# The first bf16 part of the keys is cast on ACT instead of DVE

## The chip, the cores and the metric

One core of one Trainium2 chip. The metric is the device time of one execution in microseconds. The kernel before took 319.92 us, median of three runs (319.9 to 320.2).

## The reference

Two layers over 32 sequences of 128 tokens with 128 features. All inputs are fp32.

```python
# layer 0: gated MLP with quantised activations and ternary weights
h = x * (scale[:, None, :] * rsqrt(mean(x * x) + 1e-6))      # scale = cond @ norm_w.T + 1
val, gate = split(h @ up_w.T, 2)
h = val * gelu(gate)
x = act_quant(h) @ weight_quant(down_w).T + x
...
# layer 1: attention with 16 heads of 8, and an MLP, both modulated by cond
h = layernorm(x) * g1 + b1
q, k, v = split(h @ W_qkv.T + b_qkv, 3)
attn = softmax(einsum('bhqd,bhkd->bhqk', q, k) / sqrt(8))
x = x + (einsum('bhqk,bhkd->bhqd', attn, v) @ W_o.T + b_o) * a1
x = x + (gelu_tanh((layernorm(x) * g2 + b2) @ W_f1.T + b_f1) @ W_f2.T + b_f2) * a2
```

## The kernel before, in words

The five engines each run an instruction list written out by hand; semaphores tie them together. There is no scheduler: what stands behind a waiting instruction on the same engine waits too.

The work has three parts. The first is layer 0, a pipeline of steps `s` (one sequence each, `gated_mlp(s)`). It also does the first layer norm of layer 1: POOL writes the normalised tiles (`xn_tile`, L1071), PE transposes them (L580), ACT modulates them into `feat` (L664). In a few steps listed in `EARLY_PROJ` PE projects four sequences at once to queries, keys or values: keys of group 0 in step 15 and of group 1 in step 23, values of group 0 in step 17. The second part is attention, one sequence `b` per step (`attention(b)`), in groups of four (GRP = 4) that share one projection each: queries in steps with b % 4 == 3, keys with b % 4 == 0, values with b % 4 == 2. The step with b % 4 == 1 has no projection. The third part is the MLP of layer 1, which PE fills.

Queries and keys are used as sums of bf16 parts. ACT saves a key projection as `k_f` (fp32, 128x512, L683). DVE casts it to the first part, `k_part[:, 0]` (`cast_k`, L818: a `tensor_tensor` addition of a zero that is broadcast). POOL takes the rest `k_rest` (L1026) and makes parts two and three of it (L1030, L1032). SP copies the parts by DMA into the stacked operands `k_st` (L301). Queries go the same way with a plain copy on DVE for the first part (L811), and L1016, L1018, L1022 on POOL. `cast_k` waits for the saved `k_f`, for the stacked rows of the group before (`k_stacked`), and for POOL's last part of the group before (`k_step`).

In an attention step PE computes two halves of the scores for the exponentials (`exp_scores`), the weighted values of one half of the step before and of one half of this step (`weigh`), two halves of the scores of the sequence three ahead for its maxima (`max_scores`), and a transposition of the split maxima (L434). DVE transposes the weighted values out of PSUM (`o_turn`, L900), takes the reciprocal (L903), reduces the two maxima (`mx`, L893) and transposes the normalised output back (L907). POOL splits the maxima into bf16 parts (L1040 to L1046) and multiplies by the reciprocals (`o_norm`, L1094). ACT runs the two exponentials (`probs`, L727), saves the projection between them if the step has one, and copies the transposed maxima (`m_T`, L743), which SP brings into the stacked queries (L349).

PE's matrix instructions are recorded by a helper, so most have line L274; they are told apart by their tiles (in the trace the moving operand stands first: `q_st,k_st` are scores for exponentials, `k_st,q_st` for maxima, `probs,v_pad` the weighting).

Of the kernel before, what the change touches and what calls it, by code (L numbers as in the profile page):

```python
# [10 lines left out]
ALU = mybir.AluOpType  # L11
# [3 lines left out]
P = 128  # L15
# [7 lines left out]
GRP = 4  # L23
GT = GRP * P
NG = B // GRP
# [7 lines left out]
STACKS = 3  # L33
# [40 lines left out]
def late_proj(b):  # L74

    name, ahead = {3: ("q", 9), 0: ("k", 8), 2: ("v", 2)}.get(b % GRP, (None, 0))
    g = (b + ahead) // GRP
    first = {"q": 2, "k": 2, "v": 1}.get(name, NG)
    return (name, g) if name and first <= g < NG else None
# [58 lines left out]
def build(nc, x, first, early, late, cond, out):  # L138
    x_d = x.rearrange("b t d -> t b d")
    out_d = out.rearrange("b t d -> t b d")  # L140
    with ExitStack() as ctx:
# [54 lines left out]
        zero_c, eps_c = sb("zero_c", [P, 1]), sb("eps_c", [P, 1])  # L196
# [85 lines left out]
        def k_done(g):  # L282
            return 16 * 6 * (g // STACKS + 1) + (CONST_DONE if g % STACKS else 0)
# [354 lines left out]
        def _(act):  # L638
# [28 lines left out]
            def save_projection(name, g):  # L667
                act.wait_ge(shared_mm, SHARED[name, g] + 1)
                if name == "v":
                    if g >= 2:  # L670
                        act.wait_ge(b_av, 2 * GRP * (g - 1))
                    if g == 0:
                        act.wait_ge(v_const_set, 2)
                    nc.scalar.copy(v_pad[:, g % 2, :, :, :].rearrange("p s j (i c) -> p (s j) i c", c=VPITCH // 4)[:, :, :, 0:DH],
                                   bank(MISC_BANK).rearrange("p (sj i d) -> p sj i d", i=4, d=DH)).then_inc(shared_set, 1)
                elif name == "q":
                    if g:
                        act.wait_ge(q_step, 3 * g - 2)
                    nc.scalar.activation(q_f[:, :], bank(MISC_BANK), ACT.Identity, bias=b_qk[:, 0:1]).then_inc(shared_set, 1)
                else:  # L680
                    if g:
                        act.wait_ge(k_step, 3 * g - 2)
                    nc.scalar.activation(k_f[:, :], bank(MISC_BANK), ACT.Identity, bias=b_qk[:, 1:2]).then_inc(shared_set, 1)  # L683

            def gated_mlp(s):
                if s + 1 < B:
                    scale_x(s + 1)
                if s < B:
                    n = s % 2
                    act.wait_ge(a_gate_mm, s + 1)  # L690
                    if s % GRP == 0:
                        act.wait_ge(rstd0_set, s // GRP + 1)
                    if s >= 2:
                        act.wait_ge(a_hid, s - 1)
                    nc.scalar.activation(gate[:, n, :], bank(1 + n), ACT.Gelu, scale=rstd0[:, s:s + 1]).then_inc(a_gate, 1)  # L695
                if s % GRP < 2 and s // GRP + 1 < NG:
                    g = s // GRP + 1
                    act.wait_ge(x_loaded[g], 16)
                    if g == 1:
                        act.wait_ge(ssq_set, GRP)  # L700
                    for e in range(2):
                        c = GRP * g + 2 * (s % GRP) + e
                        nc.scalar.activation(sq[:, (c % 4) * D:(c % 4 + 1) * D], tile_cols(x_tok, c), ACT.Square,  # L703
                                             accum_out=ssq[:, c:c + 1]).then_inc(sq_set, 1)
                if 0 <= s - 1 < B:
                    c, n = s - 1, (s - 1) % 2
                    act.wait_ge(a_qscale, c + 1)
                    if c >= 2:
                        act.wait_ge(a_hintT_mm, c - 1)
                    nc.scalar.activation(hrnd[:, n, :], hid[:, n, :], ACT.Copy, bias=ROUND_UP,  # L710
                                         scale=qscale[:, c % 4:c % 4 + 1]).then_inc(a_hrnd, 1)
                if 0 <= s - LN_LAG < B:
                    if s == LN_LAG:
                        act.wait_ge(mods_set, 6)
                    save_features(s - LN_LAG)
                if s in EARLY_PROJ:
                    if s == 13:
                        act.wait_ge(bias_set, 2)
                    save_projection(*EARLY_PROJ[s])

            def exps(b, r):
                n = 2 * b + r
# [8 lines left out]
            def attention(b):  # L731
                on, c = 0 <= b < B, b + LEAD - 1
                if on:
                    exps(b, 0)
                if late_proj(b):
                    save_projection(*late_proj(b))
                if on:
                    exps(b, 1)
                if 0 <= c < B:
                    act.wait_ge(shared_mm, SHARED["m", c] + 1)  # L740
                    if c >= 2:
                        act.wait_ge(m_stacked[c % 2], 16 * (c // 2))
                    nc.scalar.copy(m_T[:, c % 2, :], bank(MISC_BANK).bitcast(BF16)[0:HROWS, 0:P]).then_inc(shared_set, 1)  # L743
# [20 lines left out]
        def _(dve):  # L764
# [45 lines left out]
                    dve.wait_ge(q_step, 3 * g)  # L810
                v.tensor_copy(q_part[:, 0, :], q_f[:, :]).then_inc(q_cast, 1)  # L811

            def cast_k(g):
                dve.wait_ge(shared_set, SHARED["k", g] + 1)
                if g:
                    dve.wait_ge(k_stacked[(g - 1) % STACKS], k_done(g - 1))
                    dve.wait_ge(k_step, 3 * g)
                v.tensor_tensor(k_part[:, 0, :], k_f[:, :], zero_c[:, :].to_broadcast([P, GT]), ALU.add).then_inc(k_cast, 1)  # L818

            def gated_mlp(s):  # L820
                if 0 <= s - 2 < B:
                    c, n = s - 2, s % 2
# [58 lines left out]
                if s - 1 in EARLY_PROJ:  # L881
                    name, g = EARLY_PROJ[s - 1]
                    if name == "q":
                        cast_q(g)
                    if name == "k":
                        cast_k(g)

            def maxima(c, r):
                pair = PAIRS[OWNER[FILL_AT["max", c, r]]]
# [53 lines left out]
            def attention(b):  # L943
                if 0 <= b - 1 < B:
                    normalize(b - 1)
                if 0 <= b + LEAD < B:
                    maxima(b + LEAD, 0)
                g = (b + 8) // GRP
                if b >= 0 and b % GRP == 0 and g < NG:
                    cast_q(g)  # L950
                if b >= 0 and b % GRP == 1 and g < NG:
                    cast_k(g)
                if b == 27:
                    gate_projection(0)
                if b == 28:
                    add_residual(0, MISC_BANK)
                if 0 <= b + LEAD < B:
                    maxima(b + LEAD, 1)
                if 0 <= b - 1 < B:
                    turn_back(b - 1)  # L960
                if b == 28:
                    statistics(0)
                if b == 29:
                    gate_projection(1)
                if b == 30:
                    modulate(0, MISC_BANK)
                    add_residual(1, MISC_BANK)
                    statistics(1)
# [196 lines left out]
```

## Time and profile before

| | |
|---|---|
| median of three runs | 319.92 us |
| profiled execution | 319.64 us, span 317.8 us |
| mean granted clock of TensorE | 0.983 |
| PE busy | 279.6 us (88%) |
| DVE busy | 246.6 us (78%) |
| ACT busy | 186.3 us (59%) |
| POOL busy | 178.6 us (56%) |
| chain that ended last | PE 46%, POOL 20%, DVE 17%, issue 11%, ACT 4% |

The span runs from the first to the last instruction; the profiled execution's own time is 1.84 us longer. Busy shares are over the whole span and mix the three parts. The chain that ended last is followed back from the last instruction: at each step to what released it, or to the instruction before it on its engine. In the timeline a row has the start in us, the duration in us, engine, line, operation, tiles and shape; what stands in brackets is the idle time of the engine just before it and what ended that.

### The profile page before, as it was taken

Reading aid. Unit: us, or ns where it says so; the run is one execution under the profiler, and the core shown is the slowest. Engines: PE = TensorE matmul, PEld = TensorE weight load, DVE = VectorE, ACT = ScalarE, POOL = GpSimd, SP = SyncE. Lnnn points to the kernel's source line nnn. Section 1 sums busy time; section 2 is a strip of 40 time slices with the busy share of each in tenths; the row PEclk is TensorE's granted clock in tenths of the full one; section 3 lists DMA queues with packets and bytes.
Section 4 is the critical chain, followed back from the end, with each engine's and each line's share of the span. In section 5 each row is a group of like instructions: output and inputs, shape, how many; then the busy total and the mean of one; then the engine's idle time right before and its main releaser. Section 6 shows DMA issues by size and latency. Waiting matters only on the chain.

```text
span 317.8 us, 8220 instructions
## 1 busy us (share of the span) xinstructions
PE 279.6 (88%) x2892; PEld 154.6 (49%) x2892; DVE 246.6 (78%) x650; ACT 186.3 (59%) x347; POOL 178.6 (56%) x357
## 2 busy tenths in 40 slices
PE   3989998898989576999999989888877999999993
PEld 2454454454445344555656565655443455555441
DVE  5679997877899976598989898998955676676432
ACT  4557997687768564676677777675545222333330
POOL 8032684985896669377878696953334444322300
PEclk9999999999999997899999999999979999999999
DMA  7940000430340004335354444520000011011112
GB/s 238 327 102 4 0 1 3 120 87 2 92 116 2 0 10 113 86 78 143 93 142 104 119 108 112 149 72 8 6 3 3 0 33 33 1 35 33 33 35 66
DMA packets 26216, 21.57 MB, mean 68 GB/s; under 512 B 4384, under 2 KB 25536, under 8 KB 25920
## 3 DMA queue, kind: packets, MB, share of 16 engines
q1 hardware_dynamic: 25744, 20.37, 24.0%
q10 hardware_dynamic: 432, 0.67, 0.7%
q8 instruction: 24, 0.39, 0.6%
q14 instruction: 16, 0.13, 0.1%
HBM read 4.26 MB, written 2.10 MB: 20 GB/s over the span
## 4 chain that ended last, share of the span: by engine, by line
PE 46%; POOL 20%; DVE 17%; issue 11%; ACT 4%; DMA 1%; POOLq 0%; DVEq 0%; ACTq 0%
PE psum L274 39%; DVE mx L893 5%; POOL q_rest L1016 3%; POOL q_part L1018 3%; POOL q_part L1022 2%; POOL k_rest L1026 2%; DVE hid L838 2%; POOL o_norm L1094 2%; POOL xn_tile L1071 2%; DVE o_turn L900 1%; ACT sq L703 1%; PE psum L623 1%; DVE projT L912 1%; PE psum L460 1%; POOL m_rest L1042 1%
## 5 line engine op out<-in xcount | busy, mean ns | idle before, releaser
L893 DVE TENSOR_REDUCE mx<-psum 128x8 f32<-128x1024 f32 x64 | 75.9, 1193 | 10.5 <-PE psum L274 10.3
L727 ACT ACTIVATE probs<-psum 128x1024 f32<-128x1024 f32 x64 | 65.4, 1023 | 9.5 <-PE psum L274 7.9
L274 PE MATMUL psum<-w_early,h0T 128*128 128x512 f32 x128 | 69.3, 627 | 0.0
L760 ACT ACTIVATE g_act<-psum,w_late 128x512 f32<-128x512 f32 x32 | 22.0, 688 | 46.4 <-PE psum L274 46.4
L274 PE MATMUL psum<-probs,v_pad 128*32 128x128 f32 x1024 | 42.4, 285 | 3.3 <-DVE o_turn L900 2.8
L274 PE MATMUL psum<-h2T,w_late 128*128 128x512 f32 x64 | 31.3, 605 | 0.0
L274 PEld LDWEIGHTS psum<-probs,v_pad 128*32 128x32 f32 x1024 | 25.2, 111 | 11.0 <-ACT probs L727 4.4
L274 PE MATMUL psum<-g_act,w_late 128*128 128x512 f32 x64 | 28.8, 592 | 0.0
L838 DVE SCALAR_TENSOR_TENSOR hid<-psum,rstd,gate 128x512 f32<-128x512 f32 x32 | 23.7, 739 | 6.2 <-PE psum L274 3.7
L695 ACT ACTIVATE gate<-psum,rstd 128x512 f32<-128x512 f32 x32 | 22.0, 688 | 8.9 <-PE psum L274 8.5
L274 PE MATMUL psum<-q_st,k_st 64*128 64x128 bf16 x512 | 26.2, 224 | 0.6 <-DVE mx L893 0.5
L1071 POOL TENSOR_SCALAR xn_tile<-x_tok,mv,rstd 128x128 f32<-128x128 f32 x32 | 25.7, 809 | 1.7
L274 PE MATMUL psum<-k_st,q_st 64*128 64x128 bf16 x512 | 25.5, 220 | 0.6 <-DVE mx L893 0.6
L710 ACT ACTIVATE hrnd<-hid,qscale 128x512 f32<-128x512 f32 x32 | 22.9, 716 | 4.5 <-DVE qscale L864 4.3
L1059 POOL TENSOR_TENSOR ystep<-qstep,w_step 128x1 f32<-128x1 f32 x32 | 6.1, 192 | 31.5 <-DVE qstep L852 31.5
L840 DVE TENSOR_REDUCE amax<-hid 128x1 f32<-128x512 f32 x32 | 22.0, 686 | 1.1
L274 PEld LDWEIGHTS psum<-q_st,k_st 64*128 64x128 bf16 x512 | 15.2, 96 | 15.1 <-issue 11.4
L274 PEld LDWEIGHTS psum<-w_early,h0T 128*128 128x128 f32 x128 | 20.5, 200 | 3.1 <-issue 3.1
L274 PEld LDWEIGHTS psum<-k_st,q_st 64*128 64x128 bf16 x512 | 14.5, 94 | 13.5 <-issue 11.6
L994 DVE TENSOR_SCALAR yT<-psum,w_late,mods 128x128 f32<-128x128 f32 x32 | 10.9, 403 | 12.7 <-PE psum L274 12.7
L1100 POOL TENSOR_TENSOR var_e<-mv,eps_c 128x4 f32<-128x4 f32 x8 | 1.6, 201 | 33.7 <-DVE mv L932 33.7
L1094 POOL TENSOR_TENSOR o_norm<-o_turn,rinv 128x128 f32<-128x128 f32 x32 | 15.7, 491 | 7.9 <-DVE rinv L903 7.8
(125 smaller groups left out, 541.3 us busy)
## 6 DMA issues: line engine op xcount, KB each, us to landing
q_st<-q_part SPq DMA_DIRECT2D x48, 128.0 KB
k_st<-k_part SPq DMA_DIRECT2D x48, 128.0 KB, 2.4
x_tok<-x SPq DMA_DIRECT2D x8, 256.0 KB, 7.2
out<-out_t SPq DMA_DIRECT2D x8, 256.0 KB, 2.3
w_late<-late SPq DMA_DIRECT2D x1, 1159.5 KB, 9.1
w_early<-early ACTq DMA_DIRECT2D x2, 256.0 KB, 5.4
k_st<-k_st SPq DMA_DIRECT2D x4, 128.0 KB, 4.9
q_st<-q_st SPq DMA_DIRECT2D x4, 128.0 KB
```

What stands on the lines that cost most here:

```text
L274: return nc.tensor.matmul(o, w, m, start=start, stop=stop, skip_group_check=shares)
L695: nc.scalar.activation(gate[:, n, :], bank(1 + n), ACT.Gelu, scale=rstd0[:, s:s + 1]).then_inc(a_gate, 1)
L710: nc.scalar.activation(hrnd[:, n, :], hid[:, n, :], ACT.Copy, bias=ROUND_UP, scale=qscale[:, c % 4:c % 4 + 1]).then_inc(a_hrnd, 1)
L727: nc.scalar.activation(probs[:, n % 3, :, :, :].rearrange("p f j q -> p (f j q)"), psum[:, pair[0]:pair[1] + 1, :].rearrange("p a b -> p ( ...
L760: nc.scalar.activation(g_act[:, f, :], bank(2 + f % 2), ACT.Gelu_apprx_tanh, bias=wl("b_f1")[:, f:f + 1]).then_inc(c_gelu[f], 1)
L838: v.scalar_tensor_tensor(hid[:, n, :], bank(3 + n), rstd0[:, s:s + 1], gate[:, n, :], ALU.mult, ALU.mult).then_inc(a_hid, 1)
L840: v.tensor_reduce(amax[:, m:m + 1], hid[:, n, :], X_AXIS, ALU.max, apply_absolute_value=True).then_inc(a_amax, 1)
L893: v.tensor_reduce(mx[:, c % 2, :, r, :], psum[:, pair[0]:pair[1] + 1, :].rearrange("p f (j k) -> p f j k", j=4), X_AXIS, ALU.max, negate=T ...
L994: last = v.tensor_scalar(yT[:, s, :], bank(5)[:, s * P:(s + 1) * P], wl("b_f2"), mods[:, 5, b:b + 1], ALU.add, ALU.mult)
L1016: p.tensor_tensor(q_rest[:, :], q_f[:, :], q_part[:, 0, :], ALU.subtract).then_inc(q_step, 1)
L1071: p.tensor_scalar(xn_tile[:, n + e, :], tile_cols(x_tok, c + e), mv[:, n + e, 0:1], rstd[:, n + e:n + e + 1], ALU.subtract, ALU.mult).then ...
L1094: p.tensor_tensor(o_norm[:, :, :, :], o_turn[:, :, 0:16].rearrange("p g (e d) -> p g e d", e=2), rinv[:, :, :].unsqueeze(3).to_broadcast([ ...
```

## The change

`cast_k` moves from DVE to ACT. On DVE it was an addition of zero, on ACT it is a copy with a change of type. Its waits are the same. On ACT it stands at the end of step `s` of the first part where the step before projected keys (steps 16 and 24), and between the two exponentials of the attention step with b % 4 == 1.

```diff
+            def cast_k(g):
+                act.wait_ge(shared_set, SHARED["k", g] + 1)
+                if g:
+                    act.wait_ge(k_stacked[(g - 1) % STACKS], k_done(g - 1))
+                    act.wait_ge(k_step, 3 * g)
+                nc.scalar.copy(k_part[:, 0, :], k_f[:, :]).then_inc(k_cast, 1)
+
             def gated_mlp(s):
...
                     save_projection(*EARLY_PROJ[s])
+                if EARLY_PROJ.get(s - 1, "v")[0] == "k":
+                    cast_k(EARLY_PROJ[s - 1][1])
...
                 if late_proj(b):
                     save_projection(*late_proj(b))
+                if b % GRP == 1 and 2 <= (b + 7) // GRP < NG:
+                    cast_k((b + 7) // GRP)
                 if on:
                     exps(b, 1)
...
-            def cast_k(g):
-                dve.wait_ge(shared_set, SHARED["k", g] + 1)
-                if g:
-                    dve.wait_ge(k_stacked[(g - 1) % STACKS], k_done(g - 1))
-                    dve.wait_ge(k_step, 3 * g)
-                v.tensor_tensor(k_part[:, 0, :], k_f[:, :], zero_c[:, :].to_broadcast([P, GT]), ALU.add).then_inc(k_cast, 1)
...
-                    if name == "k":
-                        cast_k(g)
...
-                if b >= 0 and b % GRP == 1 and g < NG:
-                    cast_k(g)
```

ACT in a steady group of attention before, from the key projection's step (`k_f`) to that of the values (`v_pad`); `probs` are the exponentials, `m_T` the transposed maxima. In brackets the semaphores.

```order
L683 ACTIVATE k_f<-psum,b_qk 128x512 [waits k_step,shared_mm]
L727 ACTIVATE probs<-psum 128x1024 [waits b_av,b_s2]
L743 COPY m_T<-psum 64x128 [waits m_stacked0,shared_mm]
L727 ACTIVATE probs<-psum 128x1024 [waits b_av,b_s2] x2
L743 COPY m_T<-psum 64x128 [waits m_stacked1,shared_mm]
L727 ACTIVATE probs<-psum 128x1024 [waits b_av,b_s2]
L674 COPY v_pad<-psum 128x64x8 [waits b_av,shared_mm]
```

The same place now:

```order
L683 ACTIVATE k_f<-psum,b_qk 128x512 [waits k_step,shared_mm]
L736 ACTIVATE probs<-psum 128x1024 [waits b_av,b_s2]
L754 COPY m_T<-psum 64x128 [waits m_stacked0,shared_mm]
L736 ACTIVATE probs<-psum 128x1024 [waits b_av,b_s2]
L690 CAST k_part<-k_f 128x512 [waits k_step,k_stacked2,shared_set]
L736 ACTIVATE probs<-psum 128x1024 [waits b_av,b_s2]
L754 COPY m_T<-psum 64x128 [waits m_stacked1,shared_mm]
L736 ACTIVATE probs<-psum 128x1024 [waits b_av,b_s2]
L674 COPY v_pad<-psum 128x64x8 [waits b_av,shared_mm]
```

The two exponentials that ran one after the other have the cast with its three waits between them.

DVE at the same place before, from the query cast to the end of the step without a projection (`mx` are the maxima, `o_turn`, `rinv` and `feat` the output of the sequence before):

```order
L811 CAST q_part<-q_f 128x512
L893 TENSOR_REDUCE mx<-psum 128x2x4
L907 STREAM_TRANSPOSE feat<-o_norm 128x128
L900 STREAM_TRANSPOSE o_turn<-psum 128x256
L903 RECIPROCAL rinv<-o_turn 128x16
L893 TENSOR_REDUCE mx<-psum 128x2x4
L818 TENSOR_TENSOR k_part<-k_f,zero_c 128x512
L893 TENSOR_REDUCE mx<-psum 128x2x4
```

And now:

```order
L822 CAST q_part<-q_f 128x512
L895 TENSOR_REDUCE mx<-psum 128x2x4
L909 STREAM_TRANSPOSE feat<-o_norm 128x128
L902 STREAM_TRANSPOSE o_turn<-psum 128x256
L905 RECIPROCAL rinv<-o_turn 128x16
L895 TENSOR_REDUCE mx<-psum 128x2x4 x2
```

The two maxima of the step now stand side by side.

ACT at the end of step 16 of the first part, now (`h0T` and `gate` belong to the steps after):

```order
L717 ACTIVATE hrnd<-hid,qscale 128x512
L664 ACTIVATE feat<-psum,mods 128x128
L690 CAST k_part<-k_f 128x512
L655 ACTIVATE h0T<-psum,scale 128x128
L702 ACTIVATE gate<-psum,rstd 128x512
```

The row of the cast is new; before, `h0T` followed `feat`.

## Rows read from the trace of the kernel before

**Rows 1.** Instructions by tile (`k_part`, `o_norm`): ns min/median/max, first and last start.

```profile
L818 DVE TENSOR_TENSOR k_part<-k_f,zero_c x8: 672/676/802, 60.5 to 200.3; 128x512 bf16<-128x512 f32 x8
L1094 POOL TENSOR_TENSOR o_norm<-o_turn,rinv x32: 406/408/945, 122.6 to 243.3; 128x128 f32<-128x128 f32 x32
```

**Rows 2.** Chain of waits, 129 to 165 us: start, us on the chain, what.

```profile
155.92 0.69 POOL o_norm L1094
...
156.78 1.16 POOL q_part L1022
```

**Rows 3.** Timeline of attention, one steady group and the cast before it.

```profile
141.07 0.94 POOL L1094 TENSOR_TENSOR o_norm<-o_turn,rinv 128x128 f32<-128x128 f32 x1
...
153.33 1.02 ACT L727 ACTIVATE probs<-psum 128x1024 f32<-128x1024 f32 x1
...
154.54 1.02 ACT L727 ACTIVATE probs<-psum 128x1024 f32<-128x1024 f32 x1 [0.19 <-PE psum L274]
...
155.88 0.68 DVE L818 TENSOR_TENSOR k_part<-k_f,zero_c 128x512 bf16<-128x512 f32 x1
155.88 0.94 POOL L1094 TENSOR_TENSOR o_norm<-o_turn,rinv 128x128 f32<-128x128 f32 x1
...
156.26 0.26 ACT L743 COPY m_T<-psum 64x128 bf16<-64x128 bf16 x1 [0.69 <-PE psum L434]
...
156.48 0.64 PE L274 MATMUL psum<-probs,v_pad 128*32 128x128 f32 x16
...
159.38 0.40 PE L274 MATMUL psum<-k_st,q_st 64*128 64x128 bf16 x8
...
160.11 0.24 PE L434 MATMUL psum<-eye_b,m_part 128*64 128x128 bf16 x1 [0.33 <-POOL m_part L1046]
...
163.48 0.40 PE L274 MATMUL psum<-k_st,q_st 64*128 64x128 bf16 x8
...
163.81 0.24 PE L434 MATMUL psum<-eye_b,m_part 128*64 128x128 bf16 x1
```

**Rows 4.** Timeline of attention, the transposition behind the last key cast.

```profile
208.16 0.24 PE L434 MATMUL psum<-eye_b,m_part 128*64 128x128 bf16 x1 [0.82 <-POOL m_part L1046]
```

**Rows 5.** Timeline around step 16, and busy time per engine of one stretch.

```profile
59.03 0.71 ACT L710 ACTIVATE hrnd<-hid,qscale 128x512 f32<-128x512 f32 x1
...
59.64 0.44 ACT L664 ACTIVATE feat<-psum,mods 128x128 f32<-128x128 f32 x1
...
62.60 1.13 PE L274 MATMUL psum<-w_late,feat 128*128 128x128 f32 x8 [1.16 <-ACT feat L664]
...
63.77 0.59 ACT L674 COPY v_pad<-psum 128x512 f32<-128x512 f32 x1 [1.31 <-PE psum L274]
...
60.00:61.44 1.44, 1.44 (x11) 0.68 (x8) 1.44 (x8) 1.44 (x8) 1.34 (x2) 1.00 0.00 0
```

The last row's columns are the stretch, its length, busy us (and instructions) of PE, PE's weight loads, DVE, ACT and POOL, then the granted clock, the DMA share and GB/s.

**Rows 6.** Timeline of SP's issues, and landing times of the key rows.

```profile
150.29 0.54 SPq L301 DMA_DIRECT2D k_st<-k_part  x1
...
DMA to landing us min/median/max: 2.3/2.4/3.7
```

**Rows 7.** Layer norm tiles by tile (ns), and the timeline behind step 24.

```profile
L1071 POOL TENSOR_SCALAR xn_tile<-x_tok,mv,rstd x32: 795/799/995, 31.2 to 120.7; 128x128 f32<-128x128 f32 x32
...
93.28 0.33 PE L580 MATMUL psum<-w_first,xn_tile 128*128 128x128 f32 x1 [1.04 <-POOL xn_tile L1071]
...
93.64 0.46 ACT L664 ACTIVATE feat<-psum,mods 128x128 f32<-128x128 f32 x1 [0.98 <-PE psum L580]
```

**Rows 8.** PE's two longest waits in the timeline, and windows behind them (columns above).

```profile
122.68 0.32 PE L434 MATMUL psum<-eye_b,m_part 128*64 128x128 bf16 x1 [1.94 <-POOL m_part L1046]
...
231.55 0.22 PE L434 MATMUL psum<-eye_b,m_part 128*64 128x128 bf16 x1 [1.73 <-DVE projT L912]
...
122.50:129.20 6.70, 6.08 (x66) 4.32 (x66) 2.44 (x5) 2.92 (x5) 6.06 (x11) 0.50 0.39 104
231.70:235.10 3.40, 3.40 (x45) 2.25 (x48) 1.16 (x4) 1.44 (x3) 1.70 (x3) 0.50 0.02 5
```

## Prediction

> **What bounds the kernel now.** The granted clock and the span come first: one core, 317.8 us from first to last instruction, the profiled execution at 319.64 us, 0.28 below the median of the three runs (319.92). My sum is made against the execution and shifted by that 0.28 at the end. Then the chain of waits, then the timeline of one group of four attention steps, then the timeline around the two early casts; the windows by stage give the clock.
>
> The cast that moves runs eight times on DVE, 0.68 us each [rows 1]: twice in the first part of the kernel (steps 16 and 24 of the gated MLP), six times in attention, in the step with b % 4 == 1. DVE is busy there, but the chain of waits of a steady group does not pass through the cast. It passes through POOL: the query remainder and its second part, the split of a maximum, then the o_norm multiplication, which stands with 0.69 us on the chain, the third query part at 156.78 [rows 2], the first key remainder, the split of the next maximum, and from there to PE's transposition at 160.11, for which PE stood 0.33 us [rows 3]. Group follows group at 14.81 us: the o_norm beside the cast starts at 155.88 here and at 141.07 one group earlier [rows 3].
>
> The reader should see one pair in the timeline: the cast on DVE and o_norm on POOL start together at 155.88, and o_norm takes 0.94 us [rows 3] where the fastest takes 0.41 and the median is 0.41 too [rows 1]. So the cast costs POOL 0.53 us in the place where POOL is on the chain. The Trainium skill (SBUF — State Buffer, section Who interferes with whom) says that VectorE and GpSimd share a port pair as an exclusive lock, also when a VectorE instruction has two SBUF inputs and the other reads SBUF; by that rule the loser waits out the whole 0.68 us of the cast. The row says 0.53 and decides; with 0.68 only the last group below would gain 0.15 more.
>
> **The change, part by part.**
>
> *Removed from DVE: eight casts of 0.68 us.* As DVE time I cost this at nothing in attention: the second maximum of step b % 4 == 2, like those of steps 3 and 0, starts when PE has filled its banks, so a freer DVE waits for PE. What counts is POOL. Without the cast beside it o_norm ends 0.53 us sooner, and the third query part, the key remainder and the split behind it with it. PE's transposition at 160.11 follows. It cannot gain all of it: PE's own last scores started at 159.38, and where PE does not wait, a step later, a transposition starts 0.33 us after such scores (163.48, 163.81) [rows 3]. So it can start at 159.71: **0.40 us per group**. Bounds: the idle time that the row itself gives, 0.33, and POOL's whole 0.53. Late next is PE's own stream; in steps 3 and 0 all three projections keep PE back to back, DVE and ACT follow it, and the chain returns through DVE's maximum, the query cast and POOL's query remainder, all earlier by the same 0.40. Four groups (casts near 141, 156, 171 and 185 us) give 1.60. The last (200.3 us) has no query projection behind it: there PE waits 0.82 us for POOL at 208.16 [rows 4], so the whole **0.53** passes. The first (121 us) has no stretched o_norm, since POOL is at the layer norm tiles there; I put it at 0. Sum for attention: 1.60 + 0.53 = **2.13 us less**.
>
> *Added to ACT in attention: six casts between the two exponentials.* No row has ACT casting from SBUF. The nearest are the copy of the values from PSUM, 0.59 us, and hrnd, SBUF to SBUF with a scale, 0.71 us, whose successor starts 0.61 after it [rows 5]; the copy is nearest, since it has no scale from a tile, and with the 0.10 by which neighbours overlap it keeps ACT for about 0.5. Ends: 0.49 and 0.61. The first exponential starts at 153.33, the second at 154.54 after 0.19 of idle, and 0.69 us before the maximum's copy at 156.26 ACT idles again [rows 3]. So the second exponential comes some 0.3 us later and ends near 155.9; the weighting that reads it starts at 156.48, the copy is due at 156.26. Both are covered. If the cover were gone, each further tenth would fall on PE five times.
>
> *The wait that comes with it.* On ACT the cast waits for the landing of the previous group's last key rows, and the second exponential, the copy of the maximum and through them PE are queued behind it. That transfer is issued at 150.29 and key rows land 2.3 to 3.7 us after issue [rows 6], by 154.0 at the latest; the cast comes at about 154.25 (after an exponential of 1.02 us from 153.33, less the overlap of 0.10). Nothing, so long as landings stay under 3.9 us. POOL takes the result up only behind the third query part, and SP behind query rows of its own, so neither gains or loses by an earlier cast.
>
> *Added to ACT at step 16.* Here nothing covers it. ACT is busy 1.44 of 1.44 us between 60.00 and 61.44 [rows 5], and PE stands 1.16 us for ACT's feat before the value projection at 62.60 [rows 5]. The cast goes in ahead of all that ACT work, so PE starts later by its whole price: **0.5 us more** (0.49 to 0.61). DVE's 0.68 us gained there buys nothing, since its next product needs ACT's gate, which comes later.
>
> *Step 24.* Here a layer norm tile of POOL runs beside the cast and takes 0.995 us, the longest of its kind, where the median is 0.799 [rows 7]. POOL goes on back to back until PE's transposition at 93.28, for which PE stands 1.04 us [rows 7]. I take **0.2 us less** (0.995 - 0.799). ACT is 0.5 us later here too, but it waits 0.98 us itself before the feat at 93.64 [rows 7], which covers that. Bounds: 0.2 less, 0.5 more if that cover fails.
>
> **Sum:** 319.64 - 2.13 + 0.50 - 0.20 = 317.81 against the profiled execution; with 0.28 for the median, **318.1 us**. Bounds by the ends: all five groups at 0.53 and ACT at 0.49 give 319.92 - 2.65 + 0.49 - 0.20 = 317.6; four groups at 0.33, ACT at 0.61 and step 24 at 0.5 more give 319.92 - 1.85 + 1.11 = 319.2.
>
> **Rivals.**
> (a) *TensorE's clock falls at step 17; slower.* The granted clock is 0.5 (1.2 of 2.4 GHz) from 122.5 to 129.2 and from 231.7 to 235.1, each time after PE had stood still for long, 1.94 and 1.73 us [rows 8]. At 62.60 PE now stands 1.16 us and the clock stays up; with 0.5 more it stands 1.66. [...] In the first part PE is busy all through, so a stretch of 3.4 to 6.7 us at half clock loses half of itself, 1.7 to 3.35 us: 319.8 to 321.4, middle 320.6. For it: 1.66 is nearer to 1.73. Against: the step before is fuller than those before 120 and 230.
> (b) *The gain in attention does not come, slower by the first part alone.* If o_norm still took 0.94 beside the maximum that now follows at once on DVE, 319.92 + 0.5 = 320.4. Against: other o_norms run at 0.41 beside maxima.
> (c) *The clock does not fall at 122.5.* PE's 1.94 us of standing there ends a little sooner with a freer POOL; without the fall half of 6.7 us is gained on top: 314.7. Against: 1.94 is well above 1.73.
> (d) *Part of the gain is taken back*, by a late landing in front of the second exponential or by SP, which carries all of the queries' and keys' rows: two groups of five lost, 0.8 us, 318.9.
> (e) *ACT is slow at it.* If the cast kept ACT for 2.0 us, the second exponential would end after the weighting's 156.48; past 1.1 us (0.19 + the 0.92 from 155.56 to 156.48) every tenth is on PE. At 2.0: PE 0.9 late, less the 0.40 gained, five times, plus 2.0 at step 16: 324.4. Against: ACT's 512-wide rows take 0.59 to 0.71. [...]
>
> **How the numbers follow.** Forecast 0.58, (a) 0.19, (b) 0.05, (c) 0.07, (d) 0.09, (e) 0.02. A measurement of this kernel can tell about 0.2%, 0.64 us, from no change. The range 317.2 to 320.6 takes in the forecast with its bounds and some spread, (d), (b) and the shorter half of (a); outside stay (c), (e) and the longer half of (a), 0.19 together. The forecast's own range is 317.4 to 319.2. Faster by over 0.2% (below 319.3): the forecast, (c) and most of (d), 0.72. Within 0.2%: the shorter half of (a), (b) and the edge of (d), 0.16. Slower (above 320.6): the longer half of (a) and (e), 0.12.
>
> **What would show it.** Right: o_norm at 0.41 in every group, groups 14.4 us apart instead of 14.81, no PE wait before the transposition of step 2, an ACT cast of about 0.6 us, and the value projection of step 17 half a microsecond later after 1.66 us of standing at an unbroken clock. Wrong: a granted clock of 0.5 soon after 63 us, an exponential that waits for key rows, o_norm still at 0.9, or PE waiting in attention for ACT's second exponential.

## The result and the profile after

The changed kernel takes **317.60 us** (median of 10 runs, 315.94 to 318.35), the kernel before 319.98 us on the same chip (10 runs, 318.78 to 320.82). The ratio is 0.9919, with a 95% interval of 0.9895 to 0.9944. Ratios here and below leave out executions in a slower state of the chip, and they differ by up to 0.4% from the quotients of the medians. The prediction was 318.1 us, range 317.2 to 320.6.

| | before | after |
|---|---|---|
| profiled execution, span | 319.64 us, 317.8 us | 316.87 us, 315.1 us |
| mean granted clock of TensorE | 0.983 | 0.987 |
| steady groups of the attention apart | 14.81 us | 14.41 us |

First the instructions by tile (ns min/median/max, first and last start), to be read against [rows 1, 7]:

```profile
L690 ACT CAST k_part<-k_f x8: 606/610/619, 59.9 to 197.1; 128x512 bf16<-128x512 f32 x8
...
L1094 POOL TENSOR_TENSOR o_norm<-o_turn,rinv x32: 405/406/408, 122.6 to 240.5; 128x128 f32<-128x128 f32 x32
...
L1071 POOL TENSOR_SCALAR xn_tile<-x_tok,mv,rstd x32: 792/795/800, 31.1 to 120.8; 128x128 f32<-128x128 f32 x32
```

The cast takes 0.61 us on ACT. What counts is the third number of the other two rows. The longest of 32 `o_norm` was 0.945 us and is 0.408; the longest layer norm tile was 0.995 and is 0.800. Neither line of POOL was touched by the change. A group's median would have hidden it: the medians, 0.408 and 0.799 before, are 0.406 and 0.795 now.

Then the timeline of one steady group, to be read against [rows 3]:

```profile
152.98 1.02 ACT L736 ACTIVATE probs<-psum 128x1024 f32<-128x1024 f32 x1
...
153.90 0.61 ACT L690 CAST k_part<-k_f 128x512 bf16<-128x512 f32 x1
...
154.41 1.03 ACT L736 ACTIVATE probs<-psum 128x1024 f32<-128x1024 f32 x1
154.45 2.29 DVE L895 TENSOR_REDUCE mx<-psum 128x8 f32<-128x1024 f32 x2
...
155.53 0.41 POOL L1094 TENSOR_TENSOR o_norm<-o_turn,rinv 128x128 f32<-128x128 f32 x1
...
155.91 0.26 ACT L754 COPY m_T<-psum 64x128 bf16<-64x128 bf16 x1 [0.48 <-PE psum L434]
...
156.13 0.64 PE L274 MATMUL psum<-probs,v_pad 128*32 128x128 f32 x16
```

The cast keeps ACT for 0.51 us (153.90 to 154.41, since neighbours overlap by 0.10). The exponential behind it ends at 155.44, 0.69 us before the weighting that reads it and 0.47 us before ACT's next copy. The cast is covered. And the chain of waits of the same stretch (start, us on the chain, what):

```profile
155.36 0.23 POOL m_part L1046
155.59 0.04 issue
155.63 0.24 PE psum L434
155.87 3.56 PE psum L274 x72
159.43 0.17 PE psum L434
```

Before, the chain went on through `o_norm`, the third query part and the first key remainder on POOL to the next transposition [rows 2, 3]. Now it stays on PE for 3.56 us, and the transposition at 159.43 follows PE's own scores without a wait. PE's transpositions behind POOL stand at 155.63, 170.04 and 184.44, 14.41 and 14.40 us apart.

Timeline at the two early casts and behind the last, to be read against [rows 4, 5, 7]:

```profile
63.02 1.13 PE L274 MATMUL psum<-w_late,feat 128*128 128x128 f32 x8 [1.67 <-ACT feat L664]
...
93.46 0.33 PE L580 MATMUL psum<-w_first,xn_tile 128*128 128x128 f32 x1 [0.54 <-POOL xn_tile L1071]
...
206.03 0.24 PE L434 MATMUL psum<-eye_b,m_part 128*64 128x128 bf16 x1 [0.44 <-POOL m_part L1046]
```

At step 17 PE stands 1.67 us for ACT's `feat`, 0.51 more than before; at step 24 0.54 us for POOL's tile (1.04); and behind the last cast 0.44 us for POOL (0.82). The granted clock (windows, the column after POOL):

```profile
62.00:70.00 8.00, 6.98 (x42) 4.16 (x43) 5.53 (x19) 5.84 (x12) 6.84 (x11) 1.00 0.40 108
...
122.00:130.00 8.00, 6.87 (x75) 4.65 (x75) 2.41 (x6) 3.31 (x5) 6.41 (x13) 0.57 0.36 96
...
134.00:226.00 92.00, 86.74 (x1732) 54.61 (x1731) 82.39 (x141) 67.93 (x98) 62.48 (x158) 1.00 0.38 99
226.00:240.00 14.00, 9.22 (x152) 5.50 (x151) 8.51 (x33) 7.03 (x9) 7.24 (x13) 1.00 0.02 4
```

Behind the wait at step 17 the clock stays at 1.00. The fall at PE's long wait near 122 us is there as before. The second, from 231.7 to 235.1 [rows 8], is not, though PE stands the same 1.73 us there. That was not predicted.

The sum over the two profiles, with the start of `o_norm` as the marker: from the first stretched one (0.94 us instead of 0.41) to the one behind the last cast's group, 141.07 to 210.19 before and 141.12 to 208.06 after, 2.18 us less. Up to that stretch the changed kernel is 0.05 us later. From there to the last `o_norm` it is 0.63 us shorter (33.07 before, 32.44 after: the stretch that kept its clock). Behind it the two are equal within 0.01 us. Together 2.76 us, the difference of the two executions (319.64 and 316.87) but for rounding.

### The profile page after: what moved, and what is told of

Its sections match the earlier page's. It is cut to its first block, busy times and chain, and to the rows that moved or that the text cites. A ratio compares the mean times of both kernels' runs of the same rounds, so it can differ in the third digit from the quotient of the medians.

```text
span 315.1 us, 8220 instructions
## 1 busy us (share of the span) xinstructions
PE 278.0 (88%) x2892; PEld 153.8 (49%) x2892; DVE 241.3 (77%) x642; ACT 189.1 (60%) x355; POOL 175.1 (56%) x357
## 4 chain that ended last, share of the span: by engine, by line
PE 49%; DVE 18%; POOL 14%; issue 10%; ACT 5%; DMA 2%; SPq 1%; DVEq 0%; POOLq 0%; ACTq 0%
PE psum L274 42%; DVE mx L895 6%; POOL q_rest L1016 3%; POOL q_part L1018 2%; DVE hid L842 2%; DMA q_st<-q_part 1%; ACT sq L710 1%; POOL xn_tile L1071 1%; PE psum L623 1%; DVE projT L914 1%; DVE o_turn L902 1%; PE psum L460 1%; POOL q_part L1022 1%; ACT hrnd L717 1%; PE psum L535 1%
## 5 line engine op out<-in xcount | busy, mean ns | idle before, releaser
L1040 POOL CAST m_part<-mx 128x16 bf16<-128x16 f32 x32 | 6.3, 197 | 23.8 <-DVE mx L895 23.8
```

## The experiments

The theory: DVE's cast, a sum of two SBUF operands, holds POOL up, and POOL was on the chain; DVE's time as such costs nothing, and the early casts cost 0.3 us together. The rivals: DVE's time is what counted; the earlier cast lets the transfers start earlier; the first part or the clock made some of the difference.

Single runs of this kernel scatter by up to some 3 us either way (the kernel before: 316.0 to 323.0 us on the three chips of the table), so the verdicts below rest on the traces, one of each version, and the medians only go with them. One table holds all runs. "Start" is the time from ACT's `gate` of step s = 7 in the first part to PE's first transposition in the attention, which no fall of the clock lies in; before it is 77.96 us, in the first profile of the changed kernel 78.24. "Groups" are the distances of `o_norm` in the steps with the cast.

| version | median us | before, same chip | ratio, 95% interval | start us | groups us |
|---|---|---|---|---|---|
| attention only | 317.82 | 319.15 | 0.9955 (0.9910 to 1.0001) | 77.94 | 14.41 14.48 14.57 14.42 |
| early casts only | 320.58 | 319.15 | 1.0033 (0.9996 to 1.0070) | 78.25 | 14.81 14.72 15.52 14.41 |
| reduction added | 317.97 | 319.15 | 0.9958 (0.9927 to 0.9990) | 78.25 | 14.61 14.41 14.76 14.41 |
| sum added | 319.99 | 319.15 | 1.0004 (0.9976 to 1.0033) | 78.25 | 14.80 14.81 15.52 14.41 |
| changed kernel again | 317.65 | 319.67 | 0.9960 (0.9922 to 0.9999) | 78.32 | 14.42 14.42 14.41 14.42 |
| step 16 on DVE | 317.58 | 319.67 | 0.9942 (0.9911 to 0.9972) | 77.80 | 15.05 14.57 14.41 14.42 |
| copy on DVE | 318.60 | 319.67 | 0.9968 (0.9929 to 1.0007) | 78.01 | 14.60 14.55 14.54 15.08 |
| two casts more on ACT | 320.22 | 319.67 | 1.0019 (0.9988 to 1.0051) | 78.33 | 14.93 14.93 14.95 14.99 |
| before, filled | 317.60 | 320.30 | 0.9955 (0.9920 to 0.9989) | 77.97 | 14.80 14.82 14.82 14.81 |
| changed, filled | 315.45 | 320.30 | 0.9874 (0.9826 to 0.9923) | 78.29 | 14.42 14.41 14.42 14.41 |
| step 16 on DVE, filled | 316.37 | 320.30 | 0.9876 (0.9838 to 0.9913) | 77.79 | 14.85 14.88 14.57 14.41 |

### Half of the change

Only the six casts of the attention on ACT:

```diff
-                if EARLY_PROJ.get(s - 1, "v")[0] == "k":
-                    cast_k(EARLY_PROJ[s - 1][1])
```

(and `cast_k` on DVE again for these two.) What was expected:

> Only the six casts of the attention part are on ACT; those of steps 16 and 24 of the first part are back on DVE. Theory (the gain comes from o_norm, which POOL computes unstretched, and only in the attention; ACT's cast in step 16 costs 0.5 us on the path, that of step 24 gives 0.2 us back): groups of the attention 14.41 us apart as in the changed kernel, the v projection of step 17 as early after step 16's gate as before, xn_tile's second half in step 24 again 0.99 us; about 0.3 us faster than the changed kernel, so 317.3 us where that takes 317.6, some 2.6 us under the kernel before. Rival (the early casts contribute to the gain, since an earlier end of part 1 shifts what follows against the clock's fall at 122 us): slower than the changed kernel, 318 us or more.

Only the two early casts on ACT:

```diff
-                if b % GRP == 1 and 2 <= (b + 7) // GRP < NG:
-                    cast_k((b + 7) // GRP)
```

> Only the two early casts (steps 16 and 24) are on ACT; the six of the attention part stay on DVE. Theory: o_norm takes 0.94 us beside each of the six casts, groups stay 14.81 us apart, and step 16 costs 0.5 us, step 24 gives 0.2 us back: 0.3 us slower than the kernel before (320.3 us where that takes 320.0). Rival (part of the 2.4 us comes from the first part): as fast as before or faster, 319.5 us or less.

In the traces both halves do what the theory says, with one difference told below. The start is 77.94 us with the early casts on DVE and 78.25 with them on ACT: the early casts cost 0.3 us, in every one of the profiles. PE's wait before the value projection is 1.15 us in the one and 1.67 in the other, and the longest layer norm tile is 0.994 us in the first and 0.800 in the second. With the casts of the attention on DVE the stretched `o_norm` is back:

```profile
L1101 POOL TENSOR_TENSOR o_norm<-o_turn,rinv x32: 402/406/941, 124.0 to 243.0; 128x128 f32<-128x128 f32 x32
```

In "early casts only" this happens beside three of the six casts, not beside all six as expected. Two others start 0.11 and 0.12 us behind `o_norm`; one of them:

```profile
154.66 0.41 POOL L1101 TENSOR_TENSOR o_norm<-o_turn,rinv 128x128 f32<-128x128 f32 x1
154.77 0.84 DVE L827 TENSOR_TENSOR k_part<-k_f,zero_c 128x512 bf16<-128x512 f32 x1
155.02 1.61 POOL L1029 TENSOR_TENSOR q_part<-q_rest,q_part 128x512 bf16<-128x512 f32 x1
```

There `o_norm` keeps its 0.41 us, the sum itself takes 0.84 us instead of 0.68, and POOL's next instruction, the third query part, 1.61 us instead of 1.16. The group is 14.72 us long all the same. So an unstretched `o_norm` alone does not show that the cast is free.

The medians agree in sign only: 1.3 us under before and 1.4 us over, which together is not the change's 2.4 us less, and both intervals reach 1. They can't carry the split into halves. The attention alone was expected 0.3 us better than the whole change, which these medians can't show either.

### Is it DVE's time, POOL's stop, or the earlier cast?

Two versions leave ACT's casts as they are in the changed kernel and add to DVE, at its old place, work that nothing reads:

```diff
+                if b >= 0 and b % GRP == 1 and g < NG:
+                    idle_work(g)
...
+                v.tensor_reduce(idle_r[:, :], w_int[:, :], X_AXIS, ALU.max, apply_absolute_value=True).then_inc(idle_done, 1)
```

> The changed kernel, and DVE does work without use where its cast stood in the attention: a reduction of a constant 128 x 512 tile in SBUF to one column (686 ns for the same form in the first part), six times. It takes as much of DVE as the cast did, but reads one tensor alone. Theory (what the cast cost was POOL's o_norm beside it, not DVE's time): o_norm stays at 0.41 us, groups 14.41 us apart, time as the changed kernel, 317.6 us within 0.3. Rival (DVE's 0.68 us were on the path, by the maxima behind them or the turn of the outputs): groups 14.8 us apart again, 319.7 us. A part in between would show as a group of 14.5 to 14.7 us.

and in the other, in place of the reduction:

```diff
+                v.tensor_tensor(idle_t[:, :], w_int[:, :], zero_c[:, :].to_broadcast([P, GT]), ALU.add).then_inc(idle_done, 1)
```

> The changed kernel, and DVE does at the old place of its cast the same operation on other tiles (a sum of a constant 128 x 512 tile and a broadcast zero into a bf16 scratch tile), six times, which nothing reads. Theory (DVE's sum of two SBUF operands holds POOL's o_norm up): o_norm 0.94 us in those steps again, PE's transposition of that step waits for it again, groups 14.81 us apart, about 2.1 us slower than the changed kernel, 319.7 us. Rival (the gain comes from ACT's cast being done earlier, so that POOL's subtraction, the transfers or the stacking start earlier): groups stay 14.41 us apart and the time stays at 317.6 us, since ACT's cast is as early as in the changed kernel.

The timeline of the version with the reduction:

```profile
155.70 0.41 POOL L1105 TENSOR_TENSOR o_norm<-o_turn,rinv 128x128 f32<-128x128 f32 x1
155.70 0.67 DVE L831 TENSOR_REDUCE idle_r<-w_int 128x1 f32<-128x512 f32 x1
```

And of the one with the sum:

```profile
156.75 0.22 POOL L1057 TENSOR_TENSOR m_part<-m_rest,m_part 128x16 bf16<-128x16 f32 x1
156.93 0.94 POOL L1105 TENSOR_TENSOR o_norm<-o_turn,rinv 128x128 f32<-128x128 f32 x1
156.93 0.68 DVE L831 TENSOR_TENSOR idle_t<-w_int,zero_c 128x512 bf16<-128x512 f32 x1
```

The two differ in nothing but this instruction and the scratch tile that it writes. It takes 0.67 or 0.68 us of DVE, at the same place beside the same `o_norm`. Beside the reduction `o_norm` takes 0.41 us and groups come as close as 14.41; beside the sum it takes 0.94 and they are 14.80 and 14.81 apart, though ACT's cast is as early as in the changed kernel. So DVE's time is free there, and the earlier cast brings nothing: both rivals fall in these groups, and the medians, 317.97 and 319.99, stand 2.0 us apart. In one group each of this version and of "early casts only" (the ones of 15.52 us, where the marker itself came later) the sum met the last part of the maximum's split instead:

```profile
186.54 0.68 DVE L831 TENSOR_TENSOR idle_t<-w_int,zero_c 128x512 bf16<-128x512 f32 x1
186.70 0.60 POOL L1057 TENSOR_TENSOR m_part<-m_rest,m_part 128x16 bf16<-128x16 f32 x1
```

In these traces whatever POOL starts within the sum is held up, here 0.60 us for 0.22, directly ahead of PE's transposition.

The reduction has two longer groups, 14.61 and 14.76 us, and a group of 14.5 to 14.7 us was named beforehand as the sign that DVE's time counts in part. No POOL instruction is stretched in them, and the chain of waits of these stretches (141 to 157 us and 170 to 186 us) does not pass through the reduction. In the first it stands 3.42 us on the transfer of the maxima:

```profile
141.83 3.42 DMA q_st<-m_T
```

What lengthened the second stays open. "Attention only", without any added work, has groups of 14.48 and 14.57 us too.

### A copy on DVE in place of the sum

```diff
-                v.tensor_tensor(k_part[:, 0, :], k_f[:, :], zero_c[:, :].to_broadcast([P, GT]), ALU.add).then_inc(k_cast, 1)
+                v.tensor_copy(k_part[:, 0, :], k_f[:, :]).then_inc(k_cast, 1)
```

> The kernel before, all eight casts still on DVE, but as a copy with one operand in SBUF (0.41 us for the same form, the query cast) where it was a sum of two operands (0.68 us). What such a copy does to POOL is in no row yet, since POOL stands idle beside the query cast. Theory in its narrow form (only an instruction with two operands from SBUF holds POOL up): o_norm 0.41 us in every group, groups 14.41 us apart, no cost in step 16, about 317.1 us, 0.5 us better than the changed kernel. Wide form (any fast instruction of DVE between SBUF tiles holds POOL up for about as long as it runs): o_norm 0.6 to 0.8 us in the six steps, groups 14.5 to 14.8 us apart, 318 to 319.5 us. Rival (DVE's time counts by itself): 0.27 us less per cast, groups 14.55 us apart with o_norm still 0.94 us.

```profile
153.03 0.41 DVE L818 CAST k_part<-k_f 128x512 bf16<-128x512 f32 x1
153.04 0.67 POOL L1094 TENSOR_TENSOR o_norm<-o_turn,rinv 128x128 f32<-128x128 f32 x1
```

The narrow form falls: a copy with one operand holds POOL up as well. The wide form holds, with 0.67 us, groups of 14.54 to 14.60 (the one of 15.08 us is not explained) and 318.6 us; the reduction marks its limit, since it stops nobody. The reduction reads one operand and also writes one column where the sum and the copy write 512; no version here separates the two. `o_norm` is stretched by 0.26 us under a copy of 0.41 and by 0.53 under a sum of 0.68, in both cases DVE's duration less 0.15. Of that, about 0.1 us finds cover behind PE: 0.26 costs a group 0.13 to 0.19, 0.53 costs it 0.40. The Trainium skill (SBUF — State Buffer, section SBUF: two separate sides) states that VectorE (DVE) takes the port pair that it shares with GpSimd (POOL) for instructions with two SBUF inputs and for those in a two-port performance mode, which it says fp32 copies between SBUF tiles trigger. The Trainium skill (VectorE: DVE Perf Modes, section The perf-mode tier table) lists only the base mode for a reduction. The three rows agree on which instruction holds GpSimd up: 0.94 us beside the sum, 0.67 beside the copy, 0.41 beside the reduction.

### How much room ACT has

```diff
+                if g >= 2:
+                    for n in range(2):
+                        if 2 * (g - 2) + n:
+                            act.wait_ge(idle_done, 2 * (g - 2) + n)
+                        nc.scalar.copy(idle_t[:, :], w_int[:, :]).then_inc(idle_done, 1)
```

> The changed kernel, with two more casts of a constant 128 x 512 tile into a scratch tile, which nothing reads, right behind ACT's cast in the six steps of the attention; each takes 0.5 us more of ACT. In the changed kernel the second exponential ends at 155.44 us, PE's weighting with it starts at 156.13 us, and ACT's next work (m_T) at 155.91 us. Theory (the one cast is covered with 0.5 to 0.7 us to spare, more is not): the second exponential ends 1.0 us later, so the weighting starts 0.3 us and m_T 0.5 us later; groups 14.7 to 15.0 us apart, 1.5 to 3 us slower than the changed kernel. Rival (ACT has a whole microsecond or more to spare there): groups stay 14.41 us apart and the time stays.

```profile
155.26 1.27 ACT L697 CAST idle_t<-w_int 128x512 bf16<-128x512 f32 x2
...
156.44 1.02 ACT L743 ACTIVATE probs<-psum 128x1024 f32<-128x1024 f32 x1
...
157.51 0.64 PE L276 MATMUL psum<-probs,v_pad 128*32 128x128 f32 x16 [0.45 <-ACT probs L743]
```

PE now waits 0.45 us for the second exponential. Groups are 14.93 to 14.99 us apart, 0.52 to 0.58 more, and the median is 2.6 us above the changed kernel's. 1.2 us more on ACT (155.26 to 156.44), less 0.69 of room, is 0.49. So the one cast has cover with about 0.7 us to spare, and a third cast there would not have been free.

### The clock, and the version with step 16 on DVE

> The changed kernel itself, for a second profile and for times on the chip of the three others. In its first profile TensorE's granted clock stayed at 1.00 from 131 us on, where the profile of before has 0.50 between 231.7 and 235.1 us. Theory (the fall near 231 us is a matter of the single execution, not of the change): groups again 14.41 us apart; a fall between 228 and 236 us may or may not be there; the median is about 2.3 us under the kernel before on the same chip. Rival (the change does away with that fall): the clock is again 1.00 from 220 to 248 us.

The second profile of the same kernel, windows as above:

```profile
100.00:110.00 10.00, 6.81 (x74) 3.92 (x73) 9.93 (x31) 6.10 (x12) 6.56 (x17) 1.00 0.00 0
110.00:120.00 10.00, 9.06 (x67) 3.98 (x65) 6.41 (x11) 4.54 (x8) 5.50 (x13) 0.50 0.02 6
...
226.00:240.00 14.00, 11.08 (x142) 6.61 (x143) 7.83 (x28) 7.04 (x9) 7.20 (x11) 0.76 0.02 4
```

This execution has the clock at half from 110 to just past 120 us, and it has the fall near 230 us that the first lacked. From the third on, ACT's `gate` instructions of the two agree within 0.12 us, up to 110 us. So where the clock falls is a matter of the single execution: the 0.63 us that the first profile gained near 231 us are not the change's.

```diff
+                if s == 24:
+                    cast_k(1)
```

(in place of the early casts on ACT; step 16's cast is DVE's sum again.)

> The changed kernel with the cast of step 16 alone back on DVE; step 24's and the six of the attention stay on ACT. Theory (step 16 costs 0.5 us on the path through ACT's feat and PE's v projection, step 24's move gives 0.2 us): the v projection starts 0.4 to 0.5 us earlier, PE's idle time before it is 1.16 us again and not 1.67, groups 14.41 us apart, and the time is 0.5 us under the changed kernel (317.1 where that takes 317.6). Rival (what is won in the first part is lost at the clock's fall near 122 us or at the wait of the first attention group for its transfers): as the changed kernel.

The start is 77.80 us, 0.44 to 0.52 less than with both early casts on ACT, and PE's wait is 1.15 us. The median, 317.58, is no better than the changed kernel's 317.65. The trace shows two groups of 15.05 and 14.57 us in the attention, which alone are 0.8 us.

Last, a fill for PE: matmuls without use ahead of three transpositions, within PE's waits, in the kernel before, the changed one, and the version above.

```diff
+IDLE_FILL = {0: 3, 1: 2, 3: 7}
...
+                if c in IDLE_FILL:
+                    shared_free("m", c)
+                    for n in range(IDLE_FILL[c]):
+                        mm(bank(MISC_BANK), eye_b[:, :], w_ternT[:, :, :].rearrange("p a b -> p (a b)"))
                 pe.wait_ge(b_m, 4 * c + 4)
```

> The kernel before, with matmuls without use on TensorE ahead of three transpositions of the first attention steps (3, 2 and 7 of them, a constant bf16 128 x 512 operand into the shared bank, about 0.21 us each), inside waits for POOL of 0.73, 0.58 and 1.82 us. Of the profiles so far nine of ten have a stretch at half clock between 110 and 131 us, each execution at its own place; the profile that has none reached the attention's first steady group 1.5 to 2.7 us earlier. Theory (which stretch falls to half clock in which execution is what scatters the times, and it follows TensorE's waits there): no half clock between 110 and 131 us, 1 to 2.5 us under the kernel before, and a narrower scatter. Rival (the fill does not decide it): the fall is there again, the time is that of the kernel before, or up to 0.5 us above it if the added matmuls delay the transposition.

> The changed kernel with the same matmuls without use. Theory (the change's gain is independent of the clock: 0.40 us in each group of the attention, 0.53 us in the last, minus 0.3 us in the first part): 1.9 us under the filled kernel before of the same call, whether or not the fill does away with the fall at half clock; groups 14.41 us apart. Rival (part of the 2.4 us measured is that the change moves the fall): less than 1.2 us between the two where the fall is gone in both.

> The same matmuls without use in the version with step 16's cast on DVE and all others on ACT. Theory: 0.4 to 0.5 us under the changed kernel with the same fill, since the attention starts that much earlier (seen in the profiles: 77.80 us against 78.24 to 78.33 us from the gate of the seventh step to the first transposition), and the best of all kernels here if the fill does away with the fall. Rival: the earlier start is lost again at the first groups' transfers, no difference to the filled changed kernel.

Windows of the filled changed kernel:

```profile
110.00:120.00 10.00, 8.10 (x119) 4.15 (x116) 7.92 (x13) 6.04 (x12) 6.69 (x15) 1.00 0.03 8
120.00:122.00 2.00, 1.89 (x33) 1.08 (x30) 1.97 (x4) 1.46 (x3) 1.85 (x4) 1.00 0.66 167
122.00:130.00 8.00, 7.02 (x113) 4.39 (x112) 4.73 (x10) 4.67 (x8) 7.29 (x17) 1.00 0.42 110
```

In all three profiles the clock stays at 1.00 from 100 to 226 us. Of the ten profiles without a fill one does so too, that of the copy on DVE, although PE stood 1.92 us there:

```profile
122.64 0.24 PE L434 MATMUL psum<-eye_b,m_part 128*64 128x128 bf16 x1 [1.92 <-POOL m_part L1046]
```

So three of three against one of ten speaks for the fill, and the length of PE's wait alone does not decide whether the clock falls. From PE's first transposition to the `o_norm` of the first steady group the filled kernels take 29.04 to 29.15 us, the copy on DVE 28.93, the nine with a fall 30.27 to 32.54. Filling brings 2.7 us to the kernel before by the medians, 1.4 us by the ratio (0.4 to 2.6), and the filled changed kernel, 315.45 us (6 runs, 314.9 to 316.3), is the best median measured. With the fall at 110 to 131 us gone in both, the change is worth 2.15 us by the medians (317.60 to 315.45) and 2.4 us by the spans (315.5 to 313.1; 0.25 us of that lies behind the attention's last group, where both still have a fall). The ratio of the two ratios, 0.9874 / 0.9955, is 0.9919, the same as without the fill. The third was expected 0.4 to 0.5 us better than the filled changed kernel; it came out 0.9 us worse by the medians and equal by the ratios (0.9876 and 0.9874): the rival holds. Its start is 0.50 us earlier than that of the filled changed kernel, and groups of 14.85, 14.88 and 14.57 us lose 1.07 us. SP's row says how one of them came about:

```profile
143.10 1.83 SPq L350 DMA_DIRECT2D q_st<-m_T  x1
```

One issue of a transfer took 1.83 us where the median of this line is 0.61. It was the transfer of the maxima, for which PE then waited 0.60 us at 146.50. In the version without the fill it is the same line at 146.01 us, 1.53 us. In both profiles of the changed kernel the long issues fell on key or query rows, and their groups are 14.41 and 14.42 us all the same. Whether step 16's earlier start always puts the long issue on that transfer, or did in these two executions, stays open.

## Why the prediction was right

- *Eight casts off DVE, worth nothing as DVE's time; POOL's `o_norm` is what counts.* Right, and shown by the pair of added instructions: 0.67 us of reduction leaves two of four groups at 14.41 us and is not on the chain of the longer two, 0.68 us of sum costs 0.40 us a group.
- *0.40 us in each of four groups, capped by PE, bounds 0.33 and 0.53.* 14.81 less 14.41 is 0.40, four times. The cap was named rightly: the transposition of step 2 now follows PE's scores without a wait.
- *0.53 us in the last group.* 9.86 us from the `o_norm` beside the last cast to the third after it have become 9.30: 0.56.
- *Nothing in the first group.* Measured 0.09 to 0.18 us less between the first transposition and the `o_norm` at 122.6 (13.06 to 12.88 us; 13.24 to 13.15 in the filled pair). A small miss: the cast at 120.91 us held up POOL's first part of the maximum (L1040), which takes 0.30 us at 121.47 before and 0.20 now, and PE's wait at 122.68 went from 1.94 to 1.82 us. The prediction counted a stretched `o_norm` alone. Sum for the attention: 2.13 predicted, 2.18 found plus this.
- *ACT's cast, about 0.5 us, covered.* 0.51 us. The room was put at 1.1 us and is 0.69 behind the cast, so 1.2 in all. The version with two casts more found its end where this says.
- *The wait for the previous group's key rows costs nothing.* Right: the cast follows the first exponential at once, and the second exponential the cast. The longest landing was 4.1 us, beyond the 3.9 that the prediction allowed, without a wait in these groups.
- *Step 16: 0.5 us more.* PE's wait grew from 1.16 to 1.67 us. *Step 24: 0.2 less.* Step 24's tile is back at 0.80 us. Together 0.28 to 0.36 us in the start (77.96 to 78.24 and 78.32), against 0.3.
- *Rival (a), the clock at step 17*: didn't occur; it is at 1.00 behind a wait of 1.67 us. Both (a) and (c) were weighed by the length of PE's wait. That was the wrong measure: the clock stayed at 1.00 at waits of 1.73 us (229.44, changed kernel) and 1.92 us (122.64, copy on DVE). *Rival (c), no fall at 122 us, 314.7 us*: in single executions the fall stands elsewhere. Taken away by the fill, it leaves the changed kernel at 315.45. *Rival (d), part of it taken back by SP*: seen in other versions, not in the two profiles of the change. *Rivals (b) and (e)* are refuted by 0.41 and 0.61 us; no run shows a cast that keeps ACT for 2.0 us, the condition of (e).
- *A measurement can tell 0.2% from no change.* Too fine: the intervals here reach 0.25% to 0.5% either way. And the forecast's lower end of 317.4 us has no sum behind it; its bounds give 317.6.

By the steps the change is worth 2.13 + 0.1 - 0.3 = 1.9 us. Measured were 2.4 us by the medians (2.6 by the ratio, 1.8 to 3.4 by its ends), 2.0 on a second chip (1.3 by the ratio, 0.0 to 2.5) and 2.15 with the fill; these can't tell 1.9 from 2.4. The half microsecond by which 317.60 lies under the forecast is within that scatter and has no cause shown. What went beyond the steps in the profile was the clock near 231 us, which the second profile takes back (33.32 us there against 33.07 before and 32.44 in the first).

## What to carry to other kernels

Look at the longest instruction of a group, not at its median: a GpSimd instruction that takes twice its time only where a certain VectorE instruction runs beside it is being held up, and the price is on GpSimd's chain, not on VectorE's. Before moving work, ask which other engine the instruction stops; here a single-operand reduction of the same length stopped nobody, a copy held GpSimd up by 0.26 of its 0.41 us, and ScalarE did the same cast without touching it. Where one engine has 0.7 us of room, use it once.

## What the hardware showed that was not expected

- TensorE's clock falls at different places in executions of the same program whose instructions agree within 0.14 us from 20 us on up to that point: from 110 us in one, from 122 us in the other, and near 230 us in one and not in the other. The same wait of PE, 1.73 us, stood ahead of a fall [rows 8] and of none, and one of 1.92 us of none. Single profiles must not be compared across such a stretch.
- With some matmuls without use in three waits of PE (0.73, 0.58 and 1.82 us in the changed kernel) the clock stayed at 1.00 there in three profiles of three, without them in one of ten. By the medians that is 2.7 us for the kernel before (1.4 by the ratio) and 2.2 us for the changed one, this last across two chips.
- Where DVE's sum and `o_norm` start within 0.02 us of each other, `o_norm` was always the one held up; where `o_norm` had started 0.11 or 0.12 us earlier, the sum was (0.84 and 0.83 us for 0.68), and POOL's next instruction after it.
- A few issues on SP in each execution take longer than their 0.6 us, up to 1.7 us in the profile before and 1.9 us in the one after, on key rows; where one fell on the transfer of the maxima, it cost PE 0.60 us.
